# First attention of a four-stage Flamingo block: the order of work within an octet rearranged, activation tables loaded by early calls

## The reference, cut to what matters

```
x = x + tanh(g_xattn[0]) * L0_xattn(ctx_1024, layernorm(x), mask, ...)
def L0_xattn(x, latents, mask, ...):       # 2 heads of 64
    xn = layernorm(x, ln_x_g, ln_x_b);  ln = layernorm(latents, ln_l_g, ln_l_b)
    q  = ln @ W_q
    k, v = split(concat([xn @ W_kv, ln @ W_kv], axis=1))    # 128 keys a batch
    qn = rmsnorm(q, q_gamma) * SCALE;   kn = rmsnorm(k, k_gamma)
    sim = where(mask, qn @ kn.T, -max)
    return (softmax(sim) @ v) @ W_out + b_out
```

## Time and profile before

| | us |
|---|---|
| three runs | 1571.04, 1573.49, 1575.07 (median 1573.49) |
| profiled execution, its own time | 1572.77 |
| its span, as the profile measures it | 1571.1 |
| PE busy | 1412.5 (90%) |
| ACT busy | 1010.2 (64%) |
| DVE busy | 960.4 (61%) |
| POOL busy | 521.6 (33%) |

### The profile page before, as it was taken

The page is one execution under the profiler, slowest core; times in us unless marked ns, Lnnn a source line. Parts: engine busy times, 40 slices in busy tenths (PEclk is TensorE's granted clock), DMA queues, the critical chain, the costliest instruction groups (busy, mean ns, idle before and its releaser), DMA issues. The chain is left out here.

```text
span 1571.1 us, 33692 instructions
## 1 busy us (share of the span) xinstructions
PE 1412.5 (90%) x12013; PEld 1182.6 (75%) x12013; DVE 960.4 (61%) x2348; ACT 1010.2 (64%) x1996; POOL 521.6 (33%) x509
## 2 busy tenths in 40 slices
PE   2788579989999999999999999997999999877885
PEld 2777468878888888888888888877778888756764
DVE  7767476666666666766667666544355556645445
ACT  2777467756676676676676766645878888634442
POOL 2211134432132222322322222312234545635553
PEclk9999799999999999999999999998999999989998
DMA  8100100079990000000000000004000000022236
GB/s 237 53 4 1 33 23 2 1 134 183 34 112 2 1 2 1 2 1 2 2 1 2 1 2 1 2 1 123 1 28 12 15 17 15 30 64 65 66 85 176
DMA packets 124852, 60.46 MB, mean 38 GB/s; under 512 B 41817, under 2 KB 120113, under 8 KB 124562
## 3 DMA queue, kind: packets, MB, share of 16 engines
q1 hardware_dynamic: 120146, 48.92, 17.3%
q0 software_dynamic: 4544, 9.38, 1.8%
HBM read 28.84 MB, written 29.44 MB: 37 GB/s over the span
## 5 line engine op out<-in xcount | busy, mean ns | idle before, releaser
L1426 ACT ACTIVATE gelu<-psG,b_cols 128x512 f32<-128x512 f32 x256 | 176.3, 689 | 167.4 <-PE psG L142 154.3
L1530 PE MATMUL psDown<-w_down,hidden 128*64 128x128 f32 x4096 | 252.0, 276 | 0.6 <-DVE expert_out L1311 0.6
L1305 DVE SCALAR_TENSOR_TENSOR hidden<-psU,b_cols,gelu 128x512 f32<-128x512 f32 x256 | 189.4, 747 | 82.7 <-ACT gelu L1426 59.7
L1530 PEld LDWEIGHTS psDown<-w_down,hidden 128*64 128x64 f32 x4096 | 220.9, 137 | 18.4 <-DVE expert_out L1311 9.0
L1311 DVE TENSOR_TENSOR expert_out<-psDown,b_down 128x512 f32<-128x512 f32 x128 | 87.9, 687 | 147.9 <-PE psDown L1530 147.9
L1252 POOL TENSOR_TENSOR combine_sum<-combine_sum,combineT 128x512 f32<-128x512 f32 x48 | 61.5, 1280 | 325.5 <-ACT combineT L1440 325.5
L1281 POOL TENSOR_TENSOR dispatchT<-dispatchT,dispatch_inv 128x512 f32<-128x512 f32 x64 | 67.7, 1058 | 232.1 <-DVE dispatch_inv L1406 232.1
L1787 POOL TENSOR_TENSOR probs<-probs,row_sum 128x512 f32<-128x512 f32 x64 | 66.4, 1037 | 143.5 <-DVE row_sum L1882 142.6
L140 PE MATMUL psU<-slots_hi,w_up_hi 128*128 128x512 f32 x256 | 102.4, 400 | 7.8 <-DVE hidden L1305 6.5
L1927 ACT ACTIVATE probs<-psS,neg_max 128x128 f32<-128x128 f32 x256 | 91.4, 385 | 22.8 <-DVE neg_max L1879 16.8
L140 PE MATMUL psG<-slots_hi,w_gate_hi 128*128 128x512 f32 x256 | 103.2, 403 | 1.8 <-ACT max_c_row L1481 0.7
(11 more groups left out here) (391 smaller groups left out, 3456.3 us busy)
## 6 DMA issues: line engine op xcount, KB each, us to landing
sorted_x<-empty_rows SPq DMA_DIRECT2D x1, 12736.0 KB, 74.7
tile_rows<-sorted_x SPq DMA_DIRECT2D x78, 65.0 KB
sorted_x<-empty_rows SPq DMA_DIRECT2D x1, 4544.0 KB, 29.0
ctx<-in_ctx SPq DMA_DIRECT2D x8, 512.0 KB, 6.8
expert_ys<-expert_y SPq DMA_DIRECT2D x16, 256.0 KB, 3.6
x<-in_x SPq DMA_DIRECT2D x4, 512.0 KB, 6.2
w_gate_raw<-in_L_ffn_Wg SPq DMA_DIRECT2D x1, 2048.0 KB, 11.6
w_up_raw<-in_L_ffn_Wu SPq DMA_DIRECT2D x1, 2048.0 KB, 17.2
```

The costliest lines, as they stand in the source:

```text
L1305: dve.scalar_tensor_tensor(hid[e][:, half, :], U[half][:], bcol[:, 1, 4 * ch + 2 * e + half:][:, 0:1], gel[half][:], ALU.add, ALU.mult).th ...
L1426: act.activation(gel[half][:], G[half][:], ACT.Gelu, bias=bcol[:, 0, 4 * ch + 2 * e + half:][:, 0:1]).then_inc(s["gelu"], 1)
L1530: last = pe.matmul(DN[e * SEQ:(e + 1) * SEQ, j, :], hid[e][:, half, b * SEQ:(b + 1) * SEQ], wd[:, 2 * ch + e, half, :], start=(half == 0 a ...
```

## The change

Each edit moves instructions; none changes a result.

1. TensorE, head: the keys are made in two halves (function `keys`), the values stand between them, and the queries come last. Before: all keys, queries, values.
2. TensorE, end of a body: the transposes of the normalized keys and queries come ahead of the output projection, in the order first half of the keys, queries, second half. Before: projection, keys, queries. (In body 7 the bias rows come ahead of the transposes of the next stage's tokens.)
3. ScalarE: `kv_in` is complete after two of the three scalings. The first half of the keys is squared between the two exponentials, the copy `v` comes before the square of the second half, and in body 7 the copies `oT` come before the cast for the next stage.
4. ScalarE, tables: a square root and an exponential of one element per partition (`warm`), whose results nothing reads, stand after the second exponential and after the root of `sum_sq`. The table loads stand in front of them.
5. VectorE: `ctx_hat` of the next octet is made after the first `sum_sq` instead of after the third, and `x_hat` at the end of the body before instead of at its start, which is the same place in the queue.

The diff, cut to its core:

```diff
+            def square_keys(h, g):
+                need(act, s["sum_sq"], 3 * h)
+                need(act, s["kt"], 2 * h)
+                need(act, s["k_proj"], 2 * h + g + 1)
+                act.activation(sq_k[:, half_of(g), :], K[:, half_of(g), :], ACT.Square).then_inc(s["squared"], 1)
...
                 if has_core(o):
-                    for g in range(2):
-                        r = half_of(g)
-                        need(act, s["shifted"], 2 * o + g + 1)
-                        act.activation(pr[:, r, :], pr[:, r, :], ACT.Exp).then_inc(s["exped"], 1)
+                    probs_exp(o, 0)
                 if has_head(o):
-
-                    need(act, s["sum_sq"], 3 * h)
-                    need(act, s["kt"], 2 * h)
-                    for g in range(2):
-                        need(act, s["k_proj"], 2 * h + g + 1)
-                        act.activation(sq_k[:, half_of(g), :], K[:, half_of(g), :], ACT.Square).then_inc(s["squared"], 1)
+                    square_keys(h, 0)
+                if has_core(o):
+                    probs_exp(o, 1)
+                if has_head(o) and has_core(o):
+                    act.activation(warm[:], warm_in[:], ACT.Sqrt)
+                if has_head(o):
+                    need(act, s["v_proj"], h + 1)
+                    need(act, s["av"], h - 1)
+                    act.copy(v[1 - par][:], T[:]).then_inc(s["v_copied"], 1)
+                    square_keys(h, 1)
...
+                if has_head(o):
+                    act.activation(warm[:], warm_in[:], ACT.Exp)
                 if has_core(o):
                     need(act, s["av"], o + 1)
                     need(act, s["out_proj"], o)
+                    act.copy(oT[0:DH, :, :], S[0:DH, :, 0:SEQ])
+                    act.copy(oT[DH:P, :, :], S[DH:P, :, SEQ:P]).then_inc(s["oT_ready"], 1)
                     if o == OCTETS - 1:
                         act.wait_ge(s["first_tx"], 1)
                         act.copy(ready.lnT[0][:], X[:, 0:OP, :].rearrange("p t n -> p (t n)")).then_inc(s["first_hi"], 1)
-                    act.copy(oT[0:DH, :, :], S[0:DH, :, 0:SEQ])
-                    act.copy(oT[DH:P, :, :], S[DH:P, :, SEQ:P]).then_inc(s["oT_ready"], 1)
...
-                    if h + 1 < OCTETS:
-                        ctx_hats(h + 1)
+                        if n == 0 and h + 1 < OCTETS:
+                            ctx_hats(h + 1)
...
+                    keys(h, 0)
                     need(pe, s["x_new"], o)
                     if o == 0:
                         pe.wait_ge(s["slot_T"], 1)
                     for b in range(OB):
                         last = pe.matmul(T[:, b, :], kvin[:, b, :], w_kv[:, D:2 * D], start=True, stop=True)
                     last.then_inc(s["v_proj"], 1)
+                    keys(h, 1)
+                    need(pe, s["kv_in"], 3 * h + 3)
+                    for p in range(OP):
+                        last = pe.matmul(X[:, OP + p, :], lat[:, p, :], w_q[:], start=True, stop=True)
+                    last.then_inc(s["q_proj"], 1)
```

More of the change, by code:

```diff
@@ L800, in finish, with x_hats @@
                 keep_stats(c, dve, o, s["x_new"], s["bn"])
+            def x_hats(h):
+                need(dve, s["tx"], h)
+                for p in range(OP):
+                    t = OP * h + p
+                    last = dve.tensor_scalar(xh[:, p, :], c.x[:, t, :], c.stats[:, t, 0:1], c.inv[:, t:t + 1],
+                                             ALU.subtract, ALU.mult)
+                last.then_inc(s["x_hat"], 1)
             def ctx_hats(h):
@@ L821, in body @@
                     last.then_inc(s["first_hat"], 1)
[L822 to L831, removed]
+                if not has_core(o):
+                    x_hats(h)
+                    ctx_hats(h)
                 if isinstance(o, int) and o == 0:
@@ L927, in _, with probs_exp @@
             act.wait_ge(s["gam_ready"], 1)
-            act.wait_ge(s["zeroed"], 2)
+            act.wait_ge(s["zeroed"], 3)
+            def probs_exp(o, g):
+                r = half_of(g)
+                need(act, s["shifted"], 2 * o + g + 1)
+                act.activation(pr[:, r, :], pr[:, r, :], ACT.Exp).then_inc(s["exped"], 1)
+            def square_keys(h, g):
[3 more added lines that the diff above has]
+                act.activation(sq_k[:, half_of(g), :], K[:, half_of(g), :], ACT.Square).then_inc(s["squared"], 1)
             def body(o, par):
@@ L938, in body @@
                                    ACT.Identity, bias=cols[:, 3:4], scale=cols[:, 2:3]).then_inc(s["kv_in"], 1)
+                    act.activation(kvin[:, :, 0:SEQ], X[:, 0:OP, :].rearrange("p t (b n) -> p (t b) n", b=2),
+                                   ACT.Identity, bias=cols[:, 1:2], scale=cols[:, 0:1]).then_inc(s["kv_in"], 1)
                     act.activation(lat, X[:, OP:OB, :], ACT.Identity, bias=cols[:, 3:4], scale=cols[:, 2:3]
                                    ).then_inc(s["kv_in"], 1)
-                    act.activation(kvin[:, :, 0:SEQ], X[:, 0:OP, :].rearrange("p t (b n) -> p (t b) n", b=2),
-                                   ACT.Identity, bias=cols[:, 1:2], scale=cols[:, 0:1]).then_inc(s["kv_in"], 1)
                 if not has_core(o):
@@ L970, in body @@
                         act.copy(hi[:, r, :], raw[:, r, :]).then_inc(s["w_hi"], 1)
[L971 to L974, removed]
                 if has_core(o):
@@ L1024, in _, with keys @@
             pe.wait_ge(s["ident_ready"], 1)
+            def keys(h, g):
+                for b in range(g * OB // 2, (g + 1) * OB // 2):
+                    last = pe.matmul(K[:, b, :], kvin[:, b, :], w_kv[:, 0:D], start=True, stop=True)
+                last.then_inc(s["k_proj"], 1)
             def body(o, par):
@@ L1054, in body @@
                 if has_head(o):
-                    need(pe, s["kv_in"], 3 * h + 3)
+                    need(pe, s["kv_in"], 3 * h + 2)
                     need(pe, s["qT_ready"], h)
[L1057 to L1063, removed]
+                    keys(h, 0)
                     need(pe, s["x_new"], o)
@@ L1083, in body @@
                     last.then_inc(s["av"], 1)
+                    if o == 0:
+                        pe.wait_ge(s["row_lo"], 1)
+                    for n in range(2):
+                        pe.matmul(T[:, 0:OP, :], ones[0:1, :], over(brow[n][:], OP, 1), start=(n == 0), stop=False,
+                                  skip_group_check=True)
                     if o == OCTETS - 1:
@@ L1088, in body @@
                         last.then_inc(s["first_tx"], 1)
[L1089 to L1093, removed]
+                if has_head(o):
+                    need(pe, s["kn"], 2 * h + 1)
+                    for b in range(OB // 2):
+                        last = pe.transpose(X[:, b, :], kn[:, b, :], c.ident[:])
+                    last.then_inc(s["kt"], 1)
+                    need(pe, s["qn"], h + 1)
+                    for p in range(OP):
+                        last = pe.transpose(K[:, p, :], qn[:, p, :], c.ident[:])
+                    last.then_inc(s["qt"], 1)
+                    need(pe, s["kn"], 2 * h + 2)
+                    for b in range(OB // 2, OB):
+                        last = pe.transpose(X[:, b, :], kn[:, b, :], c.ident[:])
+                    last.then_inc(s["kt"], 1)
+                if has_core(o):
                     need(pe, s["oT_ready"], o + 1)
@@ L1098, in body @@
                     last.then_inc(s["out_proj"], 1)
[L1099 to L1111, removed]
                 if not has_core(o):
```

9 lines of the change are left out of this document (7 added, 2 removed).

## The result

| | before | after |
|---|---|---|
| median of the runs | 1572.76 us (4 runs, 1571.04 to 1575.07) | 1561.26 us (4 runs, 1556.68 to 1564.88) |
| ratio | | 0.9916, 95% interval 0.9891 to 0.9942 |
| profiled execution | 1572.77, span 1571.1 | 1556.68, span 1555.0 |
| first stage ends at | 188.48 | 171.74 |

The account below looks back on a forecast made before the run. No engine is full; a chain that changes engines bounds the octet. Gains of 10.0 (octets 2 to 6), 1.0, 2.0 and 1.05 sum to 14.05; 1572.77 less that is 1558.7, stated as 1558, range 1553 to 1565.

Parts of the forecast that it names:

- Octets 2 to 6: Five octets of the first stage: each takes 15.5 instead of 17.45 us, 2.0 gained (bounds 0.6 and 2.2), 10.0 together.
- The root "just in time": ScalarE: root starts when `probsT` is copied, 89.98, sums ending near 89.9; second `kn` ready at 92.70, 1.9 us earlier.
- Transposes ahead of the projection: TensorE, octet end: transposes end at 93.8; of ScalarE's 1.74 us idle before `kT`, 0.35 is left.
- The keys after two scalings: Head of an octet: `kv_in` complete one scaling sooner gains nothing (bounds 0 and about 0.7 us), TensorE being busy with scores.
- Octet 1: Goes from 17.73 to 16.7 us, 1.0 gained; weight casts cost 0.9 and the held-up clamp 0.3.
- Octet 0 with the head: First octet plus head of body -1: 2.0 us gained, including about 0.3 lost in the head to `ctx_hat` before sums.
- Octet 3, left as it was: Window at 96.62, clock 0.91, took 18.69 us, 1.24 more than neighbours; such a stretch was left in the forecast.
- Last octet: End of the first stage: `oT` copied at 183.35 instead of 184.41, no longer behind the other cast; 1.05 us gained.
- A: GpSimd's multiplication waits for `ctx_hat`: 0.9 us lost in each of 7 octets, 6.3 in all, 1564; chance 0.10.
- B: Only `v` gains, `kn` coming too late for the moved transposes: some 6 us in all, 1567; chance 0.07.
- C: Each table load holds ScalarE for twice 1.28 us: octet of 17.6, about 1573, no change; chance 0.06.
- D: Sums of squares come late, delaying ScalarE's root to near 93.3: octet of 18.5, slower, 1579; chance 0.04.

Follow-up runs that it names:

- the 0.97 for the values: Changed kernel with TensorE's order keys, queries, values as before and the copy `v` behind both squares: 1537.51 against 1542.83 us, 0.9963; undisturbed octets lost 0.97 us.
- The pair that differs only in what fills it: Changed kernel with values last and `v` behind the squares, 0.9963; the same plus 12 overwritten matmuls in TensorE's wait before the `probs` transposes, 0.9932.
- the first set: Runs of the changed kernel against the kernel before, giving 1561.26 against 1572.76 us; later sets had their own runs of the kernel before.

## Why the prediction came out right, step by step

Forecast 1558, measured 1561.3, inside the range; the profiled execution, from whose time the sum was made, is 1556.7 against 1558.7. By terms:

- **Octets 2 to 6, predicted 2.0 each: 2.07, without octet 3's 1.24 of low clock.** The copy of `v` earlier by 0.60: measured 0.68, and the reason held that the table is what comes last. The reordering alone brings 1.89, and the call takes 1.21 of it back. Little of that is paid, 0.23 at the transposes: GpSimd's part of their wait ends at 83.99, the copy at 84.14. The upper bound, 2.2 with calls that cost nothing, was near: 2.28 without any load. The root "just in time": it started when `probsT` was copied. Transposes ahead of the projection: of the 1.74 nothing is left, where I kept 0.35. The kernel with the projection put back loses 1.61 of the 2.07, and the one without calls 0.72. These and the 0.97 for the values add up to more than 2.07, so they are not shares: each was taken back with the others in place, and no run takes back two.
- **The keys after two scalings, at nothing.** They start at 79.06 with no idle time ahead of them, as assumed.
- **Octet 1, predicted 1.0: 1.39.** It takes 0.96 more than its neighbours, where I had 0.9 + 0.3, and the trace divides it. The casts make `probsT` 0.65 later and the product 0.67 (11.04 into the octet instead of 10.37). GpSimd's subtraction holds the clamp for 0.96 instead of 0.18, so the second `kn` is 1.45 later in all (14.75 instead of 13.30); its transposes start behind it, and ScalarE waits for them before the second half of `kT`. That is the other 0.29:

```profile
74.91 0.69 ACT L1017 ACTIVATE kT<-psX,qk_gamma 128x512 f32<-128x512 f32 x1 [0.41 <-PE psX L1126]
```

  So the clamp's 0.3 was right and the casts' 0.9 too high by 0.2; the rest of the difference is the 15.38 for an octet that I put at 15.5.
- **Octet 0 with the head, predicted 2.0: 2.03, by two wrong halves.** A low-clock stretch lay in octet 0 before (0.92) and lies in the head now: the head's window has a granted clock of 0.91 and takes 18.16, against 17.08 at 1.00 before. So the head lost 1.07 instead of 0.3, and octet 0 gained 3.10. That the sum fitted is luck.
- **Octet 3, left as it was: 1.24 more gained.** I had left such a stretch in. The idle time ahead of the transposes of `probs` was 1.19 and is 0.60, and the counts in the last section agree with the shorter wait keeping octet 3 at full clock; for this octet itself nothing more is shown. With this 1.24 the profiled execution came out 2.0 below the sum, without it it would have been within 1 us of it.
- **Last octet, predicted 1.05: 1.71.** The wait for the cast is gone as predicted: the earlier trace rows against

```profile
163.67 3.75 PE L1103 MATMUL psS<-probsT,v 128*128 128x128 f32 x16 [0.77 <-ACT probsT L993]
```

```profile
167.46 0.58 ACT L1008 COPY oT<-psS 64x512 f32<-64x512 f32 x1 [3.45 <-PE psS L1103]
```

  `oT` starts 0.04 behind the product, where it was 1.13: 1.09 gained. The product takes 3.75 at low clock, as it did before. But 0.83 is gained ahead of it, in the scores of this octet, which ran at a low clock before and don't now (from the first scores to the search for the second maxima):

```profile
168.89:172.41 3.52, 3.48 (x18) 3.18 (x18) 1.39 (x3) 1.60 (x2) 0.00 (x0) 0.61 0.00 0
```

```profile
153.86:156.55 2.69, 2.26 (x18) 2.07 (x18) 1.80 (x5) 0.00 (x0) 0.00 (x0) 1.00 0.00 0
```

  And 0.21 is lost behind it, which I had not seen: the cast for the next stage comes after `oT` now, VectorE's subtraction behind that cast ends at 170.18, and the new x, whose projection ends at 169.85, starts only at 170.09. 1.09 + 0.83 - 0.21 = 1.71. No term had the 0.83 of clock in it.

The sum of these is 16.7: 2.03 + 1.39 + 4 x 2.07 + 3.31 + 1.71.

The rivals: A falls, GpSimd's pair is 2.04 and `ctx_hat` paid, as the Trainium skill (SBUF — State Buffer, "Who interferes with whom") has it for the engine that issues second. B falls, no idle time before `kT`. C falls, from load to next start is 1.29 and 1.30, and taking both loads of an octet away saves 0.2, where a second 1.28 for each would have shown. Its neighbour, calls that cost time by where they stand, is real: in the old order they cost 0.76 an octet. D falls: the root starts 10.60 into the octet, where the bound for a loss was 13.1, and the sums are not what it starts behind. The direction of D is real: in the kernel without calls the root starts at 11.82, and the octet takes 0.72 more.

## What to carry to other kernels

When no engine is full, read what ended each idle gap and reorder so that whatever ends a gap is issued first; here the transposes ahead of the projection were worth most, and no work was removed. A table load can be moved by a call on one number, but it takes its 1.28 us plus 0.11 where the call stands: put it beside a product that ScalarE waits for anyway. Ahead of a copy that others wait for it costs (0.76 us an octet in the old order), unless another engine comes last there anyway, as GpSimd nearly does here. A wait of TensorE can cost twice, once as itself and once as the clock of the work behind it.

## What the hardware showed that I had not expected

- **The longer TensorE waits in an octet, the more often the product behind runs at about half speed.** I counted octets 2 to 6 of every trace by the idle time ahead of the transposes of `probs`. With 0.60 or less, none of 45 (nine traces) has a slow product; with 1.19, in the kernel before, one of five (3.26 us instead of 2.02); with 1.57 three of five, the clock over such an octet being 0.90; with 1.95, in the kernel with the calls alone, three of five. The kernels differ in more than this wait. The pair that differs only in what fills it is the one above: with 1.34 us more busy time on TensorE the clock stayed at 1.00 from octet 1 on. Since octets with the same wait come out either way, something else takes part, and what it is stays open.
- **An operation on 24 numbers is held until the other engine's instruction ends.** Beside GpSimd's subtraction the clamp on 24 numbers took 0.96 us instead of 0.18:

```profile
54.62 0.96 DVE L891 TENSOR_SCALAR rms<-rms 128x24 f32<-128x24 f32 x1 [1.25 <-ACT rms L998]
```

```profile
54.27 1.27 POOL L745 TENSOR_TENSOR w_up_lo<-w_up_raw,w_up_hi 128x512 fp32r<-128x512 f32 x1
```

  It ends with the subtraction, at 55.5.
- **The last stage has two lengths,** 231 and 262 us for the changed kernel, with a clock of 0.95 and 0.92 and a DMA share of 0.30 and 0.27. In the first set the kernel before had the long one too (261.1); in the others it has only medians, which move with the set. What chooses between the two stays open; the difference is larger than the whole gain, so only kernels of one set can be compared.
